# Loads that add x wait for the row of t, and ScalarE marks 18 stretches of the counts instead of 20

## The chip, the cores and the metric

The kernel runs on one core of a Trainium2 chip. The metric is the device time of one execution in microseconds (us), lower is better. TensorE multiplies matrices, VectorE and ScalarE work elementwise, GpSimd (POOL) and SyncE (SP) mainly issue transfers here.

## The reference

One layer of a graph network with attention, a spline layer behind it, a residual and a layer norm. `x` is 1250 x 512, there are 21250 edges `src -> dst` (10000 pairs both ways, and a loop on each node).

```python
HW = h @ W
s = HW @ a[:512, 0];  t = HW @ a[512:, 0]
e = leaky_relu(s[row] + t[col], 0.2)
m = segment_max(e, row);  ex = exp(e - m[row])
att = ex / segment_sum(ex, row)[row]
agg = segment_sum(att[:, None] * h[col], row)
out = silu(agg) @ base_w.T + einsum('nip,oip->no', b_splines(agg, grid), spline_w)
x = layernorm(x + out)          # h is x, row is src, col is dst
```

## The kernel before

The edges are made into a dense matrix of counts: `C[p, j, d]` says how many edges lead from node 128 j + p to node d, for ten tiles j of 128 source nodes. The work has three stages.

**Counts.** VectorE builds one-hot tiles (`hit`, `still`, `oh`, lines 540 to 590), TensorE multiplies them (line 1325) into PSUM, where 25 stretches (windows) of 50 destination nodes each lie in six banks by turns. ScalarE copies finished stretches into `C` (line 1065, ten pairs or so and single ones at the end, list `TAKEN`), and writes for each of the first `MARKED` stretches a mark `Z` (line 1070): a huge number where the count is zero, so that a maximum over `trow - Z` sees edges only. The semaphore `s_cnt` counts the copies, `s_hole` the marks. A bank may take the next stretch when the old one has been read; the wait for this stands in front of a stretch's first matmul.

**The rows of t.** At the same time TensorE works out s and t, ScalarE puts t and 0.2 t into `strow`, and SP writes them in four pieces to `t_row` in DRAM (line 410), waits for all four, and loads them back, spread over the 128 partitions: `trow` (t, line 412, semaphore `s_trow`) and `gentle` (0.2 t, line 413). SP's queue holds nothing else meanwhile.

**x in two parts.** The product with x is made of two numbers for each value: `xh`, x rounded as it is loaded, and `xl`, what is left, x - xh. For `xl` ScalarE writes minus xh (`minus_x`, line 1075, one of ten tiles after each of ten batches of edges; `s_neg` counts them), and POOL issues four loads that add x onto it in memory (lines 518 and 520): tiles 0 to 3, 4 to 6, 7 and 8, and the 98 rows of tile 9. The first signals `s_xa[0]`, the other three `s_xa[1]`. Behind them on POOL stand the loads of the weights `wh`, the first of which waits for the first aggregated tile.

**Attention.** VectorE then goes once through a loop for edges outside the bands (lines 779 to 816), in which the first tile's work is interleaved: an early maximum over the marked stretches (line 801), marks of the other stretches for tiles 0 and 1 (line 803, `NEAR`), `bent` (line 774: the leaky sums in `ex`, from gentle and trow), a late maximum over the other stretches (line 810), and then `tmax`. ScalarE takes exponentials (line 1106) and marks the other stretches of tiles 2 to 9 (`last_marks`, line 1185). TensorE transposes (line 1364) and multiplies (line 1384) for each tile three times: the high part of the weights with xh, the low part with xh, and the high part with xl. For tile 0 the product with xl comes in two parts, `sums(0, 2, 0)` for four tiles of xl, `sums(0, 2, 1)` for the other six; they wait for `s_xa[0]` and `s_xa[1]`. From there the spline layer follows (lines 1445 and 1449), in which the weights are loaded in turn.

All orders are written by hand: each engine does its instructions in the order of its program.

Of the kernel before, what the change touches and what calls it, by code (L numbers as in the profile page):

```python
# [66 lines left out]
def middle(t):  # L67


    return MID + PER_BATCH * (t // TB) + PER_TILE * (t % TB)  # L70
# [18 lines left out]
def parts_of(t):  # L89

    parts = []
    for w, lo, hi in stretches(t):
        old = min(max(reached(t, w), lo), hi) if t > FIRST_TILE[w] else lo
        parts += [(w, a, b) for a, b in ((lo, old), (old, hi)) if a < b]
    return parts
# [29 lines left out]
def build(nc, x, xT, edges, dstN, WT, a2, baseT, splT, out):  # L125
    with ExitStack() as ctx:
# [156 lines left out]

        TAKEN = [(w, 2) for w in range(0, 22, 2)] + [(22, 1), (23, 1), (24, 1)]

        MARKED, NEAR = 20, 2
        TABLE = 19

        def done(b):

            return min(TB * b + TB, NV)

        def taken(w):

            return next(k + 1 for k, (v, n) in enumerate(TAKEN) if v <= w < v + n)
# [72 lines left out]
        def lows(u):  # L368

            return sum(split_low(k) for k in range(u + 1))  # L370

        def w_source(u):
            g, h, q = units[u]
            t = baseT if q == 0 else splT[q - 1]
            return t[256 * h:256 * h + 256, :].rearrange("(c p) o -> p c o", p=128)
# [6 lines left out]
        def unit_used(u):  # L382

            if u % HU == HU - 1:
                return s_tile, 5 * (u // HU + 1)
            return s_unit, u + 1 - u // HU
# [79 lines left out]
        @block.gpsimd  # L466
        def _(e):
            e.iota(im[:, :], [[1, MV]], base=-MV // 2, channel_multiplier=0,
                   allow_small_or_imprecise_dtypes=True).then_inc(s_setup, 1)
            e.iota(mid[:, :], [[PER_BATCH, NCP // TB], [PER_TILE, TB]], base=MID, channel_multiplier=0,  # L470
                   allow_small_or_imprecise_dtypes=True).then_inc(s_setup, 1)
            e.iota(tile_of[:, :], [[1, 2]], base=0, channel_multiplier=2,
                   allow_small_or_imprecise_dtypes=True).then_inc(s_setup, 1)
            e.iota(im8[:, :], [[LANES, MV // LANES]], base=-MV // 2, channel_multiplier=0,
                   allow_small_or_imprecise_dtypes=True).then_inc(s_setup, 1)
            e.iota(lane[:, :], [[1, LANES]], base=0, channel_multiplier=0,
                   allow_small_or_imprecise_dtypes=True).then_inc(s_setup, 1)
            e.memset(nought[:, :], 0.0).then_inc(s_setup, 1)
            e.memset(ident[:, :], 0.0).then_inc(s_setup, 1)
            e.wait_ge(s_setup, SETUP["id0"])  # L480
            e.affine_select(out=ident[:, :], in_=ident[:, :], compare_op=ALU.not_equal, fill=1.0, base=0,
                            pattern=[[-1, 128]], channel_multiplier=1).then_inc(s_setup, 1)
            e.memset(xh[:, NT - 1, :].bitcast(F32), 0.0).then_inc(s_setup, 1)
            e.memset(xt0[:, :, N:RP], 0.0).then_inc(s_setup, 1)
            e.memset(bias[:, 2 * NP + 1:2 * NP + 2], BIG).then_inc(s_setup, 1)
            e.memset(ex[:, 0:3, N:RP], 0.0).then_inc(s_setup, 1)

            e.memset(half[:, :], 0.5).then_inc(s_setup, 1)
            e.memset(eps[:, :], EPS).then_inc(s_setup, 1)
            e.iota(way[:, 0, :], [[-1, 2]], base=NC, channel_multiplier=-2,  # L490
                   allow_small_or_imprecise_dtypes=True).then_inc(s_setup, 1)
            e.iota(way[:, 1, :], [[1, 2]], base=1, channel_multiplier=2,
                   allow_small_or_imprecise_dtypes=True).then_inc(s_setup, 1)
            for p in range(NP):
                e.memset(bias[:, p:p + 1], 5.5 - (p + 2)).then_inc(s_setup, 1)
            for p in range(NP):
                e.memset(bias[:, NP + p:NP + p + 1], 0.5 ** 0.5 * (5.5 - (p + 2))).then_inc(s_setup, 1)
            e.memset(bias[:, 2 * NP:2 * NP + 1], 2.0 * (1 / 6) ** 0.5).then_inc(s_setup, 1)
            e.iota(lplace[:, :, :], [[MV, LND], [0, 2]], base=MV // 2, channel_multiplier=0,
                   allow_small_or_imprecise_dtypes=True).then_inc(s_setup, 1)  # L500

            for k in range(4):
                e.memset(limit[:, 1, k:k + 1], (-1.0, 1.0, -1.0, 1.0)[k])
                e.memset(limit[:, 2, k:k + 1], (float(NC), 0.0, float(LND), 0.0)[k])
                m = e.memset(limit[:, 3, k:k + 1], (0.0, NC + 1.0, -1.0, float(LND))[k])
            m.then_inc(s_setup, 1)


            e.wait_ge(s_w, 32)
            e.wait_ge(s_setup, SETUP["rest"])  # L510
            e.dma_start(xh[:, 0:NT - 1, :], x[0:1152, :].rearrange("(w p) i -> p w i", p=128)).then_inc(s_xh, 16)
            e.dma_start(xh[0:LASTP, NT - 1, :], x[1152:N, :]).then_inc(s_xh, 16)

            for part, (lo, hi) in enumerate(zip(ADDED, ADDED[1:] + (NT - 1,))):
                e.wait_ge(s_neg, NT if hi == NT - 1 else hi)
                e.dma_start(xl[:, lo:hi, :], x[128 * lo:128 * hi, :].rearrange("(w p) i -> p w i", p=128), accum_op=ALU.add
                            ).then_inc(s_xa[min(part, 1)], 16)
            e.dma_start(xl[0:LASTP, NT - 1, :], x[1152:N, :], accum_op=ALU.add).then_inc(s_xa[1], 16)  # L520


            for u in range(NU):
                if u >= NWS:
                    e.wait_ge(*unit_used(u - NWS))
                    e.wait_ge(s_wlo, lows(u - NWS))
                elif u == 0:
                    e.wait_ge(s_agg, 1)
                elif u == 2:
                    e.wait_ge(s_agg, NT)  # L530
                e.dma_start(wh[u % NWS][:, :, :], w_source(u)).then_inc(s_wh[u % NWS], 16)  # L531
# [710 lines left out]
        def _(e):  # L1242
            def ends_along():

                e.wait_ge(s_wa, 1)
                e.wait_ge(s_tab, 9)
                e.wait_ge(s_setup, SETUP["ident"])
                e.transpose(PS[0:8, 7, 128:128 + NBLK], ends[0:NBLK, :, :].rearrange("p k j -> p (k j)"),
                            ident[0:NBLK, 0:NBLK]).then_inc(s_rt, 1)
# [52 lines left out]
            def keep_warm(n, bank=6):  # L1302

                for k in range(n):
                    e.matmul(PS[:, bank, 0:CW], nought[:, 0:128], nought[:, 0:CW], start=True, stop=True)
# [3 lines left out]
            for g, (b, n) in enumerate(GROUPS):  # L1309
                if b == BY_SCALAR:  # L1310
                    e.wait_ge(s_by, 1)
                else:
                    e.wait_ge(s_mv, g + 1 - (b > BY_SCALAR))
                e.wait_ge(s_head, g + 1)
                moved = oh8[g % RB] if IN_LANES[g] else oh_by if b == BY_SCALAR else oh[g]
                held = still[g % RB]
                for t in range(TB * b, done(b + n - 1)):
                    k, o = t - TB * b, middle(t) - REACH[b]
                    if b == BY_SCALAR and k == TB // 2:
                        keep_warm(3, 7)  # L1320
                        e.wait_ge(s_by, 2)
                    for w, lo, hi in parts_of(t):
                        if w >= 6 and lo == FIRST_OF[w] and t == FIRST_TILE[w]:
                            e.wait_ge(s_hole, taken(w - 6))
                        m = e.matmul(PS[:, w % 6, lo - CW * w:hi - CW * w], held[:, k, :], moved[:, k, lo - o:hi - o],  # L1325
                                     start=(t == FIRST_TILE[w]), stop=(t == LAST_TILE[w]))
                    m.then_inc(s_ct, 1)
                if g == 1:
                    for c in range(4):
                        w_times_a(c)  # L1330
                if g == 2:
                    wa_column()
                if g == 4:
                    ends_along()
                if g == 5:
                    most_along()
                if g in (3, 4, 5, 6):
                    st_rows(g - 3)
                if g == 9:
                    s_column()  # L1340
                if g == LOADS_AT:
                    e.wait_ge(s_tab, TABLE)
                    left = loaded(e, r_size, 4, 5, 1, LND * NC)[0]
# [177 lines left out]
```

## Time and profile before

| | |
|---|---|
| median of 3 runs | 389.68 us (388.93 to 390.03) |
| the profiled execution | 388.39 us, of which the span of the core is 386.6 |
| TensorE busy | 370.7 us (96%) |
| VectorE busy | 336.4 us (87%) |
| ScalarE busy | 255.9 us (66%) |
| POOL busy | 37.0 us (10%) |
| mean granted clock of TensorE | 0.992 |

The span is the time on the core from the first to the last instruction; all places below are counted from its start. Busy time is summed over the whole span, so it does not say which engine is waited for in a given stage.

### The profile page before, as it was taken

Reading aid. Unit: us, or ns where it says so; the run is one execution under the profiler, and the core shown is the slowest. Engines: PE = TensorE matmul, PEld = TensorE weight load, DVE = VectorE, ACT = ScalarE, POOL = GpSimd, SP = SyncE. Lnnn points to the kernel's source line nnn. Section 1 sums busy time; section 2 is a strip of 40 time slices with the busy share of each in tenths; the row PEclk is TensorE's granted clock in tenths of the full one; section 3 lists DMA queues with packets and bytes.
Section 4 is the critical chain, followed back from the end, with each engine's and each line's share of the span. In section 5 each row is a group of like instructions: output and inputs, shape, how many; then the busy total and the mean of one; then the engine's idle time right before and its main releaser. Section 6 shows DMA issues by size and latency. Waiting matters only on the chain.

```text
span 386.6 us, 5456 instructions
## 1 busy us (share of the span) xinstructions
PE 370.7 (96%) x2082; PEld 305.7 (79%) x2082; DVE 336.4 (87%) x430; ACT 255.9 (66%) x256; POOL 37.0 (10%) x92
## 2 busy tenths in 40 slices
PE   6896979999999999999999999999999999999994
PEld 3676658888888888888888888888888888888883
DVE  8997699987775789999899998988999799999445
ACT  6799454545446979774887774897667697776122
POOL 6002201000000010100101010100100101011000
PEclk9999899999999999999999999999999999999998
DMA  7918905100000047477554646442333353564202
GB/s 252 397 22 138 253 13 163 57 2 0 2 0 0 3 140 241 159 203 232 173 185 122 193 120 189 139 109 56 110 114 103 91 142 121 152 196 100 65 29 109
DMA packets 23980, 47.30 MB, mean 122 GB/s; under 512 B 1936, under 2 KB 2412, under 8 KB 23954
## 3 DMA queue, kind: packets, MB, share of 16 engines
q0 software_dynamic: 12416, 24.00, 24.2%
q1 hardware_dynamic: 11538, 22.95, 17.8%
q8 instruction: 17, 0.28, 0.3%
q14 instruction: 9, 0.07, 0.1%
HBM read 44.37 MB, written 2.57 MB: 121 GB/s over the span
## 4 chain that ended last, share of the span: by engine, by line
PE 86%; DVE 5%; DMA 4%; issue 2%; POOL 1%; ACT 1%; SPq 1%; DVEq 0%; POOLq 0%
PE PS L1449 38%; PE PS L1445 25%; PE PS L1384 18%; PE PS L1364 3%; DMA gentle<-t_row 2%; DMA t_row<-strow 1%; PE PS L1394 1%; DVE oh L574 1%; DVE still L590 1%; DVE oh L540 1%; PE PS L1459 0%; SPq L410 0%; PE PS L1325 0%; DVE hit L553 0%; DVE pat L563 0%
## 5 line engine op out<-in xcount | busy, mean ns | idle before, releaser
L1449 PE MATMUL PS<-wh,s 128*128 128x512 f32 x432 | 139.4, 390 | 0.0
L1449 PEld LDWEIGHTS PS<-wh,s 128*128 128x128 f32 x432 | 81.2, 188 | 16.8
L1445 PE MATMUL PS<-s,wh 128*128 128x482 f32 x288 | 92.8, 383 | 0.0
L1449 PE MATMUL PS<-wl,s 128*128 128x512 f32 x216 | 84.2, 390 | 0.0
L1162 ACT ACTIVATE s<-v 128x1220 fp32r<-128x1220 f32 (+1 forms) x32 | 40.0, 1250 | 37.5 <-DVE v L952 26.3
L1445 PEld LDWEIGHTS PS<-s,wh 128*128 128x128 f32 x288 | 54.6, 189 | 9.7
L1145 ACT ACTIVATE v<-xt,bias 128x1220 f32<-128x1220 f32 (+1 forms) x32 | 42.9, 1342 | 20.0 <-DVE s L962 18.0
L1445 PE MATMUL PS<-s,wl 128*128 128x482 f32 x144 | 55.2, 384 | 0.0
L946 DVE SCALAR_TENSOR_TENSOR v<-v,v 128x1220 f32<-128x1220 f32 (+1 forms) x32 | 46.4, 1450 | 7.1 <-ACT v L1148 7.1
L952 DVE SCALAR_TENSOR_TENSOR v<-v,v 128x1220 f32<-128x1220 f32 (+1 forms) x32 | 46.8, 1461 | 3.3
L962 DVE SCALAR_TENSOR_TENSOR s<-v,s 128x1220 fp32r<-128x1220 f32 (+1 forms) x32 | 46.4, 1454 | 1.3 <-ACT s L1162 1.3
L531 POOL DMA_DIRECT2D wh<-in_splT x32 | 22.9, 716 | 256.2 <-PE PS L1449 183.1
L1449 PEld LDWEIGHTS PS<-wl,s 128*128 128x128 f32 x216 | 40.5, 188 | 8.0
L948 DVE SCALAR_TENSOR_TENSOR v<-v,v 128x1220 f32<-128x1220 f32 (+1 forms) x32 | 46.5, 1453 | 0.0
L1146 ACT ACTIVATE v<-xt,bias 128x1220 f32<-128x1220 f32 (+1 forms) x32 | 42.5, 1327 | 0.0
L1148 ACT ACTIVATE v<-v,bias 128x1220 f32<-128x1220 f32 (+1 forms) x32 | 42.5, 1327 | 0.0
L1445 PEld LDWEIGHTS PS<-s,wl 128*128 128x128 f32 x144 | 27.1, 189 | 4.8
L830 DVE TENSOR_TENSOR wl<-wring,wh 128x1024 fp32r<-128x1024 f32 x24 | 29.2, 1219 | 1.5 <-issue 1.5
L1325 PEld LDWEIGHTS PS<-oh,still 128*128 128x128 bf16 x404 | 22.7, 101 | 9.7 <-DVE oh L574 7.9
L1325 PE MATMUL PS<-oh,still 128*128 128x75 fp8e4 (+38 forms) x404 | 24.6, 220 | 5.4 <-DVE oh L574 4.7
L1113 ACT CAST ph<-PS 128x1280 fp32r<-128x1280 f32 (+2 forms) x12 | 12.6, 1049 | 23.6 <-PE PS L1364 23.6
L885 DVE TENSOR_TENSOR pl<-PS,ph 128x1280 fp32r<-128x1280 f32 (+2 forms) x11 | 14.9, 1366 | 13.8 <-ACT ph L1113 13.8
(164 smaller groups left out, 429.7 us busy)
## 6 DMA issues: line engine op xcount, KB each, us to landing
wh<-in_splT POOLq DMA_DIRECT2D x32, 512.0 KB, 4.2
wring<-in_splT SPq DMA_DIRECT2D x21, 512.0 KB, 4.5
xt<-in_xT SPq DMA_DIRECT2D x1, 2500.0 KB, 12.0
xh<-in_x POOLq DMA_DIRECT2D x1, 2304.0 KB, 12.0
wh<-in_baseT POOLq DMA_DIRECT2D x4, 512.0 KB, 5.4
out<-xr SPq DMA_DIRECT2D x8, 256.0 KB
wring<-in_baseT SPq DMA_DIRECT2D x3, 512.0 KB, 3.9
xr<-in_x SPq DMA_DIRECT2D x1, 1280.0 KB, 6.4
```

The costliest lines, as they stand in the source:

```text
L946: e.scalar_tensor_tensor(out=ba, in0=bw, scalar=2.0, in1=ba, op0=ALU.subtract, op1=ALU.mult, reverse0=True).then_inc(s_a3, 1)
L948: e.scalar_tensor_tensor(out=bq, in0=bw, scalar=2.0, in1=bq, op0=ALU.subtract, op1=ALU.mult).then_inc(s_b3, 1)
L952: e.scalar_tensor_tensor(out=bw, in0=bq, scalar=2 / 3, in1=ba, op0=ALU.add, op1=ALU.min).then_inc(s_spl, 1)
L962: e.scalar_tensor_tensor(out=parts(sl, u), in0=bufs(u)[0], scalar=0.0, in1=parts(sh, u).bitcast(F32), op0=ALU.max, op1=ALU.subtract).then_ ...
L1145: e.activation(bw, agg_in, ACT.Abs, bias=bias[:, q - 1:q], scale=2.5).then_inc(s_abs, 1)
L1146: e.activation(bq, agg_in, ACT.Square, bias=bias[:, NP + q - 1:NP + q], scale=2.5 * sq2).then_inc(s_q2, 1)
L1148: e.activation(ba, bw, ACT.Square, bias=bias[:, 2 * NP:2 * NP + 1], scale=-sq6).then_inc(s_a2, 1)
L1162: e.activation(parts(sh, u), bufs(u)[0], ACT.Relu).then_inc(s_shi, 1)
L1325: m = e.matmul(PS[:, w % 6, lo - CW * w:hi - CW * w], held[:, k, :], moved[:, k, lo - o:hi - o], start=(t == FIRST_TILE[w]), stop=(t == LA ...
L1384: m = e.matmul(PS[:, 5 + j % 2, :], pp[:, j % 3, place(j, t), :], xs[:, t % NT, :], start=(i == 0 and t == 0), stop=(i == end and t == b - ...
L1445: m = e.matmul(PS[:, w, 0:TURNED], wx[:, ic, 128 * w:128 * w + 128], sx[:, ic, 0:TURNED], start=begins, stop=ends_)
L1449: m = e.matmul(PS[:, out_bank(w), :], sx[:, ic, c:c + 128], wx[:, ic, :], start=begins, stop=ends_)
```

## The change

Two constants of the program and one wait. POOL waits for `trow` before the first of its four adding loads; the loads themselves and their order stay. `MARKED` is 18: ScalarE makes no mark for the pair of stretches 18 and 19 while the counts are made, and these two stretches go with the last five, to VectorE for tiles 0 and 1 and to ScalarE's `last_marks` for the others. A stretch whose old bank has no mark any more waits for the copy (`s_cnt`); of the 25 this is stretch 24, which follows stretch 18.

```diff
-        MARKED, NEAR = 20, 2
+        MARKED, NEAR = 18, 2
...
+            e.wait_ge(s_trow, 16)
             for part, (lo, hi) in enumerate(zip(ADDED, ADDED[1:] + (NT - 1,))):
                 e.wait_ge(s_neg, NT if hi == NT - 1 else hi)
                 e.dma_start(xl[:, lo:hi, :], x[128 * lo:128 * hi, :].rearrange("(w p) i -> p w i", p=128), accum_op=ALU.add
...
                         if w >= 6 and lo == FIRST_OF[w] and t == FIRST_TILE[w]:
-                            e.wait_ge(s_hole, taken(w - 6))
+                            e.wait_ge(s_hole if w - 6 < MARKED else s_cnt, taken(w - 6))
```

POOL's program around the loads, with the semaphores that a row waits for (`a_neg` is `s_neg`, `a_trow` is `s_trow`, `t_agg` is `s_agg`); before:

```order
L512 DMA xh<-in_x 98x512
L518 DMA xl<-in_x 128x4x512 [waits a_neg]
L518 DMA xl<-in_x 128x3x512 [waits a_neg]
L518 DMA xl<-in_x 128x2x512 [waits a_neg]
L520 DMA xl<-in_x 98x512
L531 DMA wh_107<-in_baseT 128x2x512 [waits t_agg]
```

and now (the new line shifts all line numbers behind it by one):

```order
L512 DMA xh<-in_x 98x512
L519 DMA xl<-in_x 128x4x512 [waits a_neg,a_trow]
L519 DMA xl<-in_x 128x3x512 [waits a_neg]
L519 DMA xl<-in_x 128x2x512 [waits a_neg]
L521 DMA xl<-in_x 98x512
L532 DMA wh_107<-in_baseT 128x2x512 [waits t_agg]
```

The order is the same; the first load has one more wait, and the other three stand behind it.

ScalarE's program at the end of the counts, where the pairs of stretches 18 and 19 and 20 and 21 are copied (`t_ct` counts the count matmuls); before:

```order
L1065 CAST C<-PS 128x10x100 [waits t_ct]
L1070 ACTIVATE Z<-PS,bias 128x10x100
L1075 ACTIVATE xl<-xh 128x512 [waits s_xh]
L1087 ACTIVATE s_part<-PS 128x3 [waits t_sc]
L1087 ACTIVATE s_part<-PS 128x3
L1087 ACTIVATE s_part<-PS 128x2 x2
L1065 CAST C<-PS 128x10x100 [waits t_ct]
```

and now:

```order
L1066 CAST C<-PS 128x10x100 [waits t_ct]
L1076 ACTIVATE xl<-xh 128x512 [waits s_xh]
L1088 ACTIVATE s_part<-PS 128x3 [waits t_sc]
L1088 ACTIVATE s_part<-PS 128x3
L1088 ACTIVATE s_part<-PS 128x2 x2
L1066 CAST C<-PS 128x10x100 [waits t_ct]
```

The mark is gone, and what stood behind it follows the copy.

VectorE's program in its loop, from the early maximum (`scrap` with its result `top`) to the late one; before:

```order
L764 ISA scrap,top<-trow,Z 128x1000 [waits v_touch,a_scol,a_hole,a_trow]
L764 ISA top 128x1
L719 TENSOR_SCALAR Z<-C 128x2x250 [waits a_cnt]
L774 SCALAR_TENSOR_TENSOR ex<-gentle,s_part,trow 128x512 [waits a_gentle,a_scol,a_trow]
L808 ISA [waits v_near,t_ovp,v_early]
L808 TENSOR_TENSOR C<-C,PS 128x10x32
L764 ISA scrap,top<-trow,Z 128x250
```

and now:

```order
L765 ISA scrap,top<-trow,Z 128x900 [waits v_touch,a_scol,a_hole,a_trow]
L765 ISA top 128x1
L720 TENSOR_SCALAR Z<-C 128x2x350 [waits a_cnt]
L775 SCALAR_TENSOR_TENSOR ex<-gentle,s_part,trow 128x512 [waits a_gentle,a_scol,a_trow]
L809 ISA [waits v_near,t_ovp,v_early]
L809 TENSOR_TENSOR C<-C,PS 128x10x32
L765 ISA scrap,top<-trow,Z 128x350
```

The instructions and their waits are the same; 100 columns have moved from the early maximum to the late one, and the marks of two tiles have grown from 250 columns to 350.

## Rows read from the trace of the kernel before

**Rows 1.** The page, chain that ended last: share of the span by engine.

```profile
PE 86%; DVE 5%; DMA 4%; issue 2%; POOL 1%; ACT 1%; SPq 1%; DVEq 0%; POOLq 0%
```

**Rows 2.** Chain of waits: start, length (us), what; three pieces from 29 to 47.

```profile
29.22 0.66 SPq L410
...
31.10 5.70 DMA t_row<-strow
...
37.22 9.38 DMA gentle<-t_row
```

**Rows 3.** Timeline of VectorE: start, length (us), instruction, [idle before it, releaser].

```profile
35.94 0.46 DVE L553 TENSOR_TENSOR hit<-im,gk 128x544 f16<-128x544 f16 x1 [2.16 <-issue]
...
41.50 0.32 DVE L793 TENSOR_TENSOR one_moving<-im,kk 128x320 bf16<-128x320 f16 x1
44.82 1.20 DVE L764 CUSTOM_DVE_ANT_0 scrap<-trow,Z 128x1000 bf16<-128x1000 f32 x1 [3.00 <-DMA trow<-t_row]
...
45.95 0.29 DVE L719 TENSOR_SCALAR Z<-C 128x500 bf16<-128x500 uint16 x1
46.72 0.75 DVE L774 SCALAR_TENSOR_TENSOR ex<-gentle,s_part,trow 128x512 f32<-128x512 f32 x1 [0.48 <-DMA gentle<-t_row]
```

**Rows 4.** Timeline of ScalarE: marks, the last copies, the cast after last marks.

```profile
38.12 1.19 ACT L1070 ACTIVATE Z<-PS,bias 128x1000 bf16<-128x1000 f32 x1
...
43.58 1.07 ACT L1065 CAST C<-PS 128x500 uint16<-128x500 f32 x2 [0.38 <-PE PS L1325]
...
57.17 2.13 ACT L1185 ACTIVATE Z<-C,bias 128x250 bf16<-128x250 uint16 x2
60.21 1.23 ACT L1113 CAST ph<-PS 128x1280 fp32r<-128x1280 f32 x1 [0.90 <-PE PS L1364]
```

**Rows 5.** Timeline of TensorE (PE matmuls, PEld weight loads): counts, products with xl, transposes.

```profile
38.79 5.25 PE L1325 MATMUL PS<-oh,still 128*128 128x211 fp8e4 x74 [1.84 <-DVE oh L574]
...
55.72 2.45 PE L1384 MATMUL PS<-xl,ph 128*128 128x512 f32 x10
...
58.83 1.10 PEld L1364 LDWEIGHTS PS<-ident,ex 128*128 128x128 f32 x10 [0.18 <-DVE ex L863]
```

**Rows 6.** Tile xl: POOL's issues, ns min/median/max, first and last start (us).

```profile
L518 POOL DMA_DIRECT2D xl<-in_x x3: 1194/1290/1352, 28.7 to 40.1; - x3
L520 POOL DMA_DIRECT2D xl<-in_x x1: 1363/1363/1363, 40.9 to 40.9; - x1
```

**Rows 7.** DMA queues in 29.5:30.7, 30.7:34.5, 34.5:36.5, 37:40.5, 41.5:45: packets, MB, share.

```profile
q1 hardware_dynamic: 4, 0.00, 0.9%
...
q0 software_dynamic: 260, 0.53, 102.0%
...
q1 hardware_dynamic: 12, 0.01, 1.7%
...
q0 software_dynamic: 311, 0.61, 104.1%
...
q1 hardware_dynamic: 231, 1.09, 99.7%
```

**Rows 8.** DMA issues of the whole run: KB each, us from issue to landing.

```profile
wring<-in_baseT SPq DMA_DIRECT2D x3, 512.0 KB, 3.9
...
xl<-in_x POOLq DMA_DIRECT2D x1, 1024.0 KB, 8.9
...
trow<-t_row SPq DMA_DIRECT2D x1, 640.0 KB, 8.0
...
ei<-in_edges SPq DMA_DIRECT2D x1, 176.0 KB, 2.4
```

**Rows 9.** Windows: stretch, its length, busy us (instructions), PEclk, DMA share, GB/s.

```profile
29.00:30.00 1.00, 1.00 (x19) 0.78 (x16) 1.00 (x5) 1.00 (x3) 1.00 (x1) 1.00 0.08 16
39.50:42.50 3.00, 3.00 (x36) 2.88 (x35) 2.32 (x8) 1.57 (x6) 2.11 (x2) 0.50 1.12 281
46.00:48.00 2.00, 2.00 (x11) 0.89 (x10) 1.52 (x6) 0.00 (x0) 0.00 (x0) 1.00 1.14 208
```

## The prediction

> **What bounds the kernel now.** I read the page's chain of work first: 86% of it is TensorE [rows 1]. From about 54 us to the end TensorE hardly pauses, so whatever makes that stream begin sooner or later moves the end by as much. Then I read the chain of waits just ahead of the stream: two transfers stand in it, the last row written to t_row (issued at 31.10, landed 5.70 later) and `gentle` (issued at 37.22, landed at 46.60) [rows 2]. VectorE's timeline shows what they hold up: it is through with the one-hots at 41.82, waits 3.00 for trow, does the early maximum (1.20) and the near marks (0.29), waits 0.48 for gentle, and at 46.72 begins `bent`, from which everything up to the stream follows [rows 3]. The other input of this stretch, the counts, is complete when ScalarE's last copy ends, 43.58 + 1.07 = 44.65 [rows 4]. So the rows of t are late by about two microseconds against the counts.
>
> Why they are late is seen in the DMA queues. POOL issues the loads that add x at 28.74 and on to 40.87 [rows 6]; their packets are in q0, those of t_row, trow and gentle in q1. The first write of t_row has its 4 packets through between 29.5 and 30.7. From 30.7 to 34.5 there are q0 packets alone, at 102% of the 16 engines, and the other 12 packets of t_row come only between 34.5 and 36.5. It happens again to trow: issued at 36.81, it has no packet from 37.0 to 40.5, where q0 alone fills the engines, and q1 gets them (99.7%) from 41.5 on [rows 7]. So a q1 packet here waits for what q0 has queued before it.
>
> **The wait on POOL.** It holds back four loads. Behind them on POOL stand only the weight loads, which wait for the first aggregated tile anyway, so nothing else is late by it; SP's queue is not changed, but what it issues no longer meets the loads. Its effect in steps:
>
> *The rows of t.* The last write is issued at 31.10. Its packets should come some 1.4 later, as those of the first write did (issued at 29.22 [rows 2], through by 30.7 [rows 7]), and it lands between 33.0 (0.5 after its packets) and 33.5 (2.4 after issue, as `ei` does [rows 8]). Then trow: 640 KB. The lower end is 3.9, what a 512 KB load takes [rows 8]; the upper is 1.5 to the first packet, 0.655 MB at the 311 GB/s that q1 had from 41.5 to 45 (1.09 MB in 3.5 us [rows 7]) = 2.1, and 0.9 for landing = 4.5. So trow lands at T = 36.9 to 38.0; I take 37.5, against 44.8 before (36.81 + 8.0). gentle, issued 0.4 behind it, takes its turn on the same engines: some 2 us more, 39.5, against 46.60.
>
> *VectorE.* The early maximum no longer waits: it runs from 41.85 to about 43 in what was idle time. The near marks need all counts, 44.65. They take 0.29 for 2x250 [rows 3]; 2x350 at the same price per element is 0.41, so they end at 45.1. bent starts there, 46.72 - 45.1 = 1.6 sooner. The late maximum grows from 250 to 350 columns; at the early one's 1.20 for 1000 that is 0.12, on the path. The sum at the row maximum, and so at TensorE's stream: **1.5 us sooner**. What is late next is the counts, then TensorE's own stream.
>
> *The loads themselves.* I put them at nothing only if they land before TensorE wants them. It wants the second part (all four loads) at the fifth of ten matmuls on xl, 55.72 + 4 x 0.23 = 56.6, the weights 0.2 before: 56.4; 1.5 sooner that is 54.9 [rows 5]. Alone, the loads move 208 GB/s at 114% share [rows 9]. At that the first one's 1.05 MB take 5.0 of its 8.9 from issue to landing [rows 8], so 3.9 are start and landing; all four together, 2.56 MB, take 12.3, and I put 12.8, that is 200 GB/s, to leave room for pauses between the loads. Together T + 16.7: 54.2 for T = 37.5, and 53.6 to 54.7 over the bounds. They are hidden with 0.7 to spare (0.2 at the upper bound); each microsecond beyond that is paid in full, but for 0.18 that TensorE waits soon after in any case [rows 5]. The first part lands after 8.9, at 46.4, far ahead of the 54.0 at which it is wanted.
>
> **The marks.** Gone is one Z mark of ScalarE, 1.19 at 38.12 [rows 4]. It gives nothing: ScalarE waits for TensorE before the next counts. It comes back later as 800 more elements in the last marks, 2.13 for 2000, so 0.85 more; ahead of the next cast ScalarE stands idle 0.90 there [rows 4], which hides it (if the cover were short, tile 1's cast and TensorE behind it would be late by the rest, at most 0.3). TensorE's wait for the bank of stretch 24 now goes by the copy instead of the mark; that copy stands ahead of the mark, which began at 38.12, and the matmuls that need it belong to the run of 74 that TensorE begins at 38.79 [rows 5]: nothing. The costs of near marks and late maximum, 0.1 each, are in the sum above.
>
> The profiled execution took 388.39, so it would take 386.9; it lies 1.29 under the median of the runs shown, and from that, 389.68, I predict **388.2**. From runs between 388.93 and 390.03, 0.3% (1.17 us) is about what can be told from no change.
>
> **A rule that speaks against it.** While POOL issued the first load, from 29 to 30 us, VectorE was busy all the time, and POOL's issue ended after 1.35 as usual [rows 6, 9]; the load at 40.87, half of it beside an idle VectorE, took 1.36. So VectorE did not hold POOL up. The Trainium skill (SBUF — State Buffer, section "SBUF: two separate sides") says that GpSimd writes the descriptors of such a DMA itself and is locked out while VectorE runs an instruction that takes both port pairs; by that rule, if VectorE's instructions here are such, loads held together into VectorE's busiest stretch could stand still there. The rows do not bear it out, and the sum goes by the rows.
>
> **The rivals.**
> *The rows of t come no sooner* (slower). If the write lands at 36.8 as before, because t_row itself is slow and not because of q0, trow follows 4.2 later, T = 41.0, and the loads end at 57.7. TensorE then stands still from 54.9, 2.8 less 0.18 = 2.6; against 1.5 gained that is 1.1 lost. Before, after a wait of 1.84 for VectorE, its granted clock was 0.50 (1.2 GHz) for the 3 us from 39.5 [rows 5, 9]; another such stretch costs 1.5 more: 392.3, or 390.8 without. The point from which it decides is T = 39.9, where the stall eats the gain. Against it: the first write's packets in rows 7, which went through before q0 was busy. 7 in 100.
> *The loads are late by a little.* T between 38.7 and 39.9, or a slower q0: 388.5 to 389.7. The spare 0.7 is thin. 13 in 100.
> *gentle meets the loads.* They are issued when trow lands, gentle perhaps still on its way; were it held as trow was held from 37 to 40.5, it would land 3.5 to 5 later, 43 to 44.5 or, if later still, behind the counts, with up to all of the gain lost: 388.5 to 389.7. Against it: gentle was issued 0.4 behind trow and needs its engines for 2, and the loads spend a part of their 3.9 before their first packets. 8 in 100.
> *POOL is held up by VectorE* (slower): as the rule above would have it, issue waits until 42.95, the early maximum's end; the loads end at 43 + 16.7 = 59.7, a stall of 4.8 less 0.18, so 3.1 lost: 392.8. 2 in 100.
> *The counts end sooner too.* Before its last three groups VectorE stands 2.16 in front of a `hit` [rows 3] for values it loads into registers. If the loads of x slow that, VectorE and TensorE gain up to 2, TensorE also the half clock behind its wait, and the time is then set by the landing at 54.2: 56.4 - 54.2 + 0.2 = 2.4 sooner, 387.3 (386.7 for T = 36.9). No row shows that these values come through the DMA engines. 10 in 100.
>
> **How the numbers follow.** The forecast has the other 60 in 100, by itself 387.8 to 388.6. 0.3% under the median is 388.5: nearly all of the forecast and the last rival, and a little of the two small delays, 0.62 faster; the two slower rivals and a clock lost in a small stall, 0.11; the rest, 0.27, the same. The range takes in the two delays and the sooner counts, 386.9 to 389.8, and leaves out the two slower rivals.
>
> **What would show it.** Right: no q0 packet until trow lands; t_row's packets within 2 us of their issue; trow landed by 38.5 and gentle by 41; the early maximum at about 41.9 without a wait; near marks waiting for the counts at 44.7; bent at 45.1; no pause of TensorE ahead of its matmuls on xl; ScalarE's last marks about 3 us and its cast still released by TensorE. Wrong: a wait of TensorE for a DMA at 55 us, or a trow that still takes 8 us with q0 empty.

## The result and the profile after

The changed kernel takes 385.69 us (median of 7 runs, 385.38 to 387.50) against 389.03 for the kernel before (7 runs, 388.32 to 390.03), run beside it. The ratio of the means, 386.36 to 389.14, is 0.9928, with a 95% interval of 0.9904 to 0.9953. That is 0.72% or 2.8 us faster. The forecast was 1.5 us faster (388.2, range 386.9 to 389.8): the direction was right, the gain about half of what came, and the median lies under the range. Two single runs of the sections below, one of the kernel before at 395.47 and one of the fifth experiment at 483.97, had a lower mean clock than the others and are left out of all ratios.

The seven runs fall into two groups: four at 385.4 to 385.7, with a mean granted clock of TensorE of 0.996 to 0.999, and three at 387.4 to 387.5, with 0.992. The profiled execution, 387.50 with a span of 385.7, is one of the second group, so it is only 0.9 shorter than the 388.39 of the profiled execution before; the fifth experiment comes to that.

First the page's chain that ended last, its share by engine, and the chain of waits from 34 to 60 us. Answers to [rows 1, 2].

```profile
PE 85%; DMA 9%; ACT 4%; POOL 1%; DVE 1%; SPq 0%; issue 0%; DVEq 0%
37.42 2.45 POOL xl L519 x2
39.87 14.11 DMA xl<-in_x
53.98 0.04 issue
54.02 3.50 PE PS L1385 x10
```

DMA has gone from 4% to 9%. t_row and gentle are gone from the chain; the last of the four adding loads, issued at 39.87 and landed at 53.98, now releases TensorE. The timeline of VectorE (start, length, instruction, idle before it and releaser), as in [rows 3]:

```profile
33.70 0.44 DVE L554 TENSOR_TENSOR hit<-im,gk 128x544 f16<-128x544 f16 x1
...
39.49 1.08 DVE L765 CUSTOM_DVE_ANT_0 scrap<-trow,Z 128x900 bf16<-128x900 f32 x1
...
41.67 0.34 DVE L720 TENSOR_SCALAR Z<-C 128x700 bf16<-128x700 uint16 x1 [1.09 <-ACT C L1066]
41.92 0.75 DVE L775 SCALAR_TENSOR_TENSOR ex<-gentle,s_part,trow 128x512 f32<-128x512 f32 x1
```

The early maximum waits no more for trow. But the `hit` before it has also moved, from 35.94 to 33.70, and its wait of 2.16 is gone: all VectorE's work from there on is 2.2 sooner. `bent` begins at 41.92 instead of 46.72. ScalarE's timeline, as in [rows 4], and TensorE's, as in [rows 5]:

```profile
39.05 2.59 ACT L1066 CAST C<-PS 128x1000 uint16<-128x1000 f32 x4
...
52.48 2.80 ACT L1186 ACTIVATE Z<-C,bias 128x350 bf16<-128x350 uint16 x2
59.34 1.23 ACT L1114 CAST ph<-PS 128x1280 fp32r<-128x1280 f32 x1 [4.06 <-PE PS L1365]
```

```profile
37.30 3.72 PE L1326 MATMUL PS<-oh,still 128*128 128x211 fp8e4 x74 [0.36 <-DVE still L591]
...
51.00 1.07 PE L1385 MATMUL PS<-xl,ph 128*128 128x512 f32 x4
54.02 1.79 PE L1385 MATMUL PS<-xl,ph 128*128 128x512 f32 x6 [1.96 <-DMA xl<-in_x]
...
57.32 1.99 PE L1365 MATMUL PS<-ident,ex 128*128 128x128 f32 x10
```

The counts end at 39.05 + 2.59 = 41.64, 3.0 sooner than the 44.65 of before. Half of that is TensorE's last run of 74 count matmuls, which begins 1.5 sooner, and half that the run takes 3.72 instead of 5.25. TensorE then comes to the second part of xl so soon that it stands still for 1.96. The queues in 30.7:34 and 37:40.5, the landings, and two windows (stretch; length; busy PE, PEld, DVE, ACT, POOL; granted clock; DMA share; GB/s), as in [rows 7 to 9]:

```profile
q1 hardware_dynamic: 12, 0.01, 0.7%
...
q0 software_dynamic: 4, 0.01, 1.4%
```

```profile
trow<-t_row SPq DMA_DIRECT2D x1, 640.0 KB, 4.4
gentle<-t_row SPq DMA_DIRECT2D x1, 625.0 KB, 5.6
xl<-in_x POOLq DMA_DIRECT2D x1, 196.0 KB, 14.1
```

```profile
37.30:41.00 3.70, 3.70 (x76) 3.66 (x77) 3.27 (x9) 3.65 (x10) 3.58 (x4) 1.00 0.30 78
54.10:60.10 6.00, 6.00 (x25) 4.99 (x26) 3.09 (x6) 1.94 (x2) 0.00 (x0) 0.72 0.01 3
```

The last 12 packets of t_row pass between 30.7 and 34 (before, between 34.5 and 36.5), and trow, issued at 32.69, lands 4.4 later instead of 8.0. TensorE's granted clock is full in the stretch of the last counts, where it had been half (1.2 of 2.4 GHz) in [rows 9]; behind TensorE's new wait it is 0.72 over 6 us.

### The profile page after: what moved, and what is told of

The parts are those of the page before. It is cut to its first block, busy times and chain, and to the rows that moved or that the text cites. A ratio compares the mean times of both kernels' runs of the same rounds, so it can differ in the third digit from the quotient of the medians.

```text
span 385.7 us, 5456 instructions
## 1 busy us (share of the span) xinstructions
PE 371.6 (96%) x2082; PEld 305.9 (79%) x2082; DVE 336.4 (87%) x430; ACT 255.4 (66%) x255; POOL 37.1 (10%) x92
## 4 chain that ended last, share of the span: by engine, by line
PE 85%; DMA 9%; ACT 4%; POOL 1%; DVE 1%; SPq 0%; issue 0%; DVEq 0%
PE PS L1450 38%; PE PS L1446 25%; PE PS L1385 17%; DMA xl<-in_x 4%; DMA xh<-in_x 3%; PE PS L1365 3%; DMA av<-in_a 2%; ACT Z L1071 1%; ACT xl L1076 1%; ACT C L1066 1%; PE PS L1395 1%; POOL xl L519 1%; PE PS L1460 0%; POOL xh L511 0%; DVE st L978 0%
## 5 line engine op out<-in xcount | busy, mean ns | idle before, releaser
L1163 ACT ACTIVATE s<-v 128x1220 fp32r<-128x1220 f32 (+1 forms) x32 | 40.0, 1250 | 37.5 <-DVE v L953 26.3
L1450 PEld LDWEIGHTS PS<-wl,s 128*128 128x128 f32 x216 | 40.5, 188 | 8.0
L1385 PE MATMUL PS<-xl,ph 128*128 128x512 f32 x100 | 25.9, 404 | 2.0 <-DMA xl<-in_x 2.0
L1326 PEld LDWEIGHTS PS<-oh,still 128*128 128x128 bf16 x404 | 21.4, 97 | 6.8 <-DVE oh L575 5.9
```

What stands on the lines that cost most here:

```text
L1163: e.activation(parts(sh, u), bufs(u)[0], ACT.Relu).then_inc(s_shi, 1)
L1385: m = e.matmul(PS[:, 5 + j % 2, :], pp[:, j % 3, place(j, t), :], xs[:, t % NT, :], start=(i == 0 and t == 0), stop=(i == end and t == b - ...
L1450: m = e.matmul(PS[:, out_bank(w), :], sx[:, ic, c:c + 128], wx[:, ic, :], start=begins, stop=ends_)
```

## The experiments

Theory A: the values that VectorE and TensorE load into registers before the last groups of edges are slow while the adding loads' packets are under way; the wait on POOL takes the packets out of that place, so the counts end sooner too. Theory B: the mark that ScalarE no longer makes lets the counts end sooner. A third question (C) was what sets the end now: the landing of xl, or something behind it. A measure for C in every trace is where TensorE begins its products of tile 1 with xh (61.49 before, 60.62 now): in all 17 profiled executions the measured time is that place plus 326.7 to 326.9 us, so what differs between these kernels differs ahead of it. Diffs are against the changed kernel unless the text says otherwise. Three kernels do other arithmetic: in the seventh and the fifteenth the loads do not add, so `xl` holds x and not x - xh; the sixth takes five sizes as constants that the others read from the data.

**One: the wait alone.**

```diff
-        MARKED, NEAR = 18, 2
+        MARKED, NEAR = 20, 2
```

> The wait on POOL alone, MARKED stays 20. Theory A (VectorE's register values come slowly while the adding loads fill the DMA engines; without them the counts end 3 us sooner, and TensorE then waits for the loads): as the change, VectorE's 2.16 us in front of its hit is gone, the counts end near 41.7, TensorE waits for xl until about 54.0, 385.4 to 387.5 us. Theory B (the mark that ScalarE no longer makes lets the counts end sooner): the counts end near 44 and most of the gain is gone, 388 us or more.

Measured: 385.82, ratio 0.9919 (0.9901 to 0.9938). `hit` at 33.70 has no wait. From the timelines of ScalarE, VectorE and TensorE:

```profile
40.07 2.56 ACT L1066 CAST C<-PS 128x1000 uint16<-128x1000 f32 x4
...
42.66 0.29 DVE L720 TENSOR_SCALAR Z<-C 128x500 bf16<-128x500 uint16 x1 [0.95 <-ACT C L1066]
...
54.18 1.65 PE L1385 MATMUL PS<-xl,ph 128*128 128x512 f32 x6 [1.28 <-DMA xl<-in_x]
```

The whole gain is there with all marks made, so B falls as its cause. The mark does make the last copies 1.0 later (they run to 42.63, against 41.64), which TensorE's wait for xl swallows: tile 1's products begin at 59.15, 2.3 sooner than before.

**Two: the marks alone.**

```diff
-            e.wait_ge(s_trow, 16)
             for part, (lo, hi) in enumerate(zip(ADDED, ADDED[1:] + (NT - 1,))):
```

> MARKED = 18 alone, POOL does not wait. Theory A: trow lands at 44.8 and gentle at 46.6 as before, VectorE's 2.16 us stays; the late maximum is 0.1 longer: 389.0 to 389.3 us, no difference from before that can be told. Theory B: the counts end about 3 us sooner, though trow hides it; VectorE's 2.16 us is gone.

Measured: 390.21, ratio 1.003 (1.0017 to 1.0043), a little slower, where no difference was expected. VectorE's timeline, and TensorE's last counts:

```profile
36.21 0.46 DVE L553 TENSOR_TENSOR hit<-im,gk 128x544 f16<-128x544 f16 x1 [2.43 <-issue]
...
48.51 0.75 DVE L774 SCALAR_TENSOR_TENSOR ex<-gentle,s_part,trow 128x512 f32<-128x512 f32 x1 [1.71 <-DMA gentle<-t_row]
```

```profile
39.05 3.73 PE L1325 MATMUL PS<-oh,still 128*128 128x211 fp8e4 x74 [2.11 <-DVE oh L574]
```

ScalarE, one mark ahead, has minus x ready sooner, POOL issues the third adding load at 39.41 instead of 40.12, and gentle now takes 11.2 to land. So it looks as if a saving on ScalarE releases a transfer into the way of another; the two were not tried apart. One more thing is to be seen here: after a wait of 2.11 TensorE's 74 matmuls take 3.73, at the full clock, while in [rows 5] they take 5.25 after 1.84. So the half clock of the kernel before is not there in every execution that has the wait.

**Three: POOL waits for the write of t_row only.** `s_tline` counts the four writes of t_row.

```diff
-            e.wait_ge(s_trow, 16)
+            e.wait_ge(s_tline, 64)
```

> POOL waits for the written t_row (the semaphore on which SP issues trow), not for the landed trow: its loads are issued at 32.7 instead of 37.4. If TensorE's wait at 52 to 54 us is for the loads alone (theory A), they land near 49.5, the wait is gone, TensorE's matmuls on xl run through at 51, and the time is 383 to 384 us, if gentle is not held up. If q0's packets push gentle back (packets of q0 from about 35.7, gentle's still under way), gentle lands up to 5 us later, at 43, and 1 to 2 us of that is lost: 385 us. Theory C (the end is set by something behind xl, such as the transposes of tile 1): no faster than the change's faster runs, 385.4.

Measured: 384.83, ratio 0.9891 (0.9873 to 0.9908), about 1 us under the changed kernel. TensorE:

```profile
52.82 1.66 PE L1385 MATMUL PS<-xl,ph 128*128 128x512 f32 x6 [0.74 <-DMA xl<-in_x]
```

The loads land 1.2 sooner, at 52.8, not the 4.4 by which they are issued sooner (32.98 for 37.42), and not at 49.5 as expected: now their packets stand behind those of trow and gentle and begin at 38.5, as those of t_row and trow stood behind the loads before. The landing of xl is what TensorE waits for, and moving it moves the time (C: the landing). Tile 1's products begin at 57.80, 3.7 sooner than before, and the profiled time, 384.69, is 3.7 shorter.

**Four: POOL waits until VectorE has its values** (the eighth `hit` of the one-hots), and for nothing else.

```diff
-            e.wait_ge(s_trow, 16)
+            e.wait_ge(s_hit, 8)
```

> POOL waits for VectorE's eighth hit, the first one behind VectorE's register values, at 34.1: 3 us sooner than trow lands, and behind the issue of trow and gentle. Theory A: register values and rows of t are out of the way, the loads land near 50.9, just ahead of the 51.7 at which TensorE wants them; no wait of TensorE, no half clock: 383.3 to 383.8 us. Theory C: 385.4 or more.

Measured: 385.54, ratio 0.9905 (0.9887 to 0.9924): no better than the change, and the expectation missed. TensorE no longer waits for xl, but its last counts are late:

```profile
38.32 5.24 PE L1326 MATMUL PS<-oh,still 128*128 128x211 fp8e4 x74 [1.37 <-DVE oh L575]
```

Its wait is put down to an `oh` that VectorE makes from 37.20 to 37.84, but in the changed kernel the same matmuls begin at 37.30, beside it. TensorE loads one register value at this place, and the loads' first packets are now just there; the half clock (5.24 for the 74, as in [rows 5]) follows its wait. That this value is what was slow is argued from the place; six, which has no such value, bears it out.

**Five: TensorE kept busy in its wait**, by nine matmuls of zeros behind the first part of xl, ahead of the wait.

```diff
             sums(0, 2, 0)
+            keep_warm(9)
             sums(0, 2, 1)
```

> The change, with nine idle matmuls (0.21 us each, into a bank not yet in use) ahead of TensorE's wait for the second part of xl, 2 us of work in place of standing still. If the 387.4 us runs differ from the 385.5 us runs by TensorE's clock alone, all runs are near 385.5 now and the granted clock behind the wait stays 1.00. If they differ by when the loads land, 387.4 us appears again.

Measured: 385.66 over three runs (385.51 to 385.81), ratio 0.9914 (0.9893 to 0.9936). Window 54.1 to 60.1:

```profile
54.10:60.10 6.00, 6.00 (x32) 4.77 (x32) 4.39 (x7) 3.64 (x3) 0.90 (x2) 1.00 0.04 9
```

The clock is full where it was 0.72, and none of the three runs is near 387.4. Together with the clocks of the seven runs (0.992 in each of the slower three) this says that the second group of the changed kernel's runs is the half clock behind the wait for xl: 1.9 us between the groups, of which 1.6 is seen in the trace (from the second part of xl to tile 1's products it is 6.60, and 4.97 in one, at the full clock). That the nine matmuls are what keeps the clock up is not shown: in ten, without them, none of six runs is near 387.4 either.

**Six: the kernel before, with constants in place of register values** (the values are the same, so the work is).

```diff
-                    first, tiles, first_win, many, left = (
-                        within(v, *ends) for v, ends in zip(loaded(e, r_size, 0, 5, 0, LND * NC), (
-                            (0, NC), (1, NC + 1), (0, LND - 1), (1, LND), (1, LND * NC))))
+                    first, tiles, first_win, many, left = NC, 1, LND - 1, 1, 1
...
-                    left = loaded(e, r_size, 4, 5, 1, LND * NC)[0]
+                    left = 1
```

> The kernel before with the five values of VectorE's loop and the one of TensorE's written into the program as constants, not loaded into registers (the loops run once, as they do with these inputs). Theory A (register values slowed by the loads): VectorE's 2.16 us in front of its hit is gone, the counts end near 41.7 to 42.5, but trow still lands at 44.8 and gentle at 46.6, so the time stays at 388.5 to 389.3. Theory D (VectorE waits there for something else that the transfers slow): the 2.16 us stays and the counts end at 44.7.

Measured: 388.91, ratio 1.0002 (0.9991 to 1.0012). VectorE:

```profile
33.69 0.44 DVE L553 TENSOR_TENSOR hit<-im,gk 128x544 f16<-128x544 f16 x1
...
45.03 1.20 DVE L762 CUSTOM_DVE_ANT_0 scrap<-trow,Z 128x1000 bf16<-128x1000 f32 x1 [5.50 <-DMA trow<-t_row]
```

The 2.16 before `hit` are the register values (VectorE's wait on the semaphore in front of them is kept), and the counts end at 42.36. TensorE, without its one value, begins its last counts at 36.85 and has no wait; it begins them at 37.30 in the changed kernel and at 38.32 in four. Alone that is worth nothing: the early maximum waits 5.50 for trow instead of 3.00. Only with the rows of t out of the way does it pay, and the wait on POOL does both.

**Seven: the kernel before, with loads that do not add.**

```diff
-                e.dma_start(xl[:, lo:hi, :], ..., accum_op=ALU.add
+                e.dma_start(xl[:, lo:hi, :], ...
```

> The kernel before with the four loads of x as plain loads, without adding (so xl holds x, and the results are others). If it is the adding that fills the engines, the same bytes take about half the time (some 400 GB/s in place of 208), t_row's last write and trow land 2 to 3 us sooner each, and 1 to 1.5 us is gained: 387.5 to 388 us. If any load in q0 does the same harm, t_row lands at 36.8 and trow at 44.8 as before: 389 us.

Measured: 384.83, ratio 0.9908 (0.9876 to 0.9941), some 3 us better than expected: `hit` is on time as well. The queue in 32:33.5, and VectorE:

```profile
q0 software_dynamic: 294, 0.60, 123.3%
```

```profile
33.70 0.44 DVE L553 TENSOR_TENSOR hit<-im,gk 128x544 f16<-128x544 f16 x1
```

The plain load moves 0.60 MB in 1.5 us, 400 GB/s, in the very stretch ahead of `hit`, and `hit` has no wait. Bytes alone do not slow the values here; loads that add do. trow takes 4.1 here, without any wait on POOL.

**Eight: the second part of xl last** of tile 0's products (`end = 2` closes the sum there).

```diff
-                end = 2 if j else 1
+                end = 2
...
-            sums(0, 2, 1)
             sums(0, 1, 0)
             turn(1)
             sums(0, 1, 1)
+            sums(0, 2, 1)
```

> The change, with TensorE's second part on xl moved behind the low products and the transposes of tile 1. Theory A: TensorE no longer stands still from 52.1 to 54.0; it waits about 1 us for VectorE's weights of tile 1 at 54.1 instead, and finishes tile 0 about 0.9 us sooner: 384.5 us, with the clock kept. If the loads are not the bound there, 385.4 to 387.5 as the change.

Measured: 384.95, ratio 0.99 (0.9879 to 0.9921), near the 384.5 of theory A.

```profile
54.46 1.31 PE L1365 MATMUL PS<-ident,ex 128*128 128x128 f32 x10 [1.13 <-DVE ex L864]
```

The wait for the loads is gone from TensorE; a smaller one for VectorE, 1.13, stands in its place.

**Nine: three, with four of the low products ahead of xl's second part.**

```diff
-            e.wait_ge(s_trow, 16)
+            e.wait_ge(s_tline, 64)
...
-            sums(0, 2, 1)
             sums(0, 1, 0)
+            sums(0, 2, 1)
             turn(1)
```

> The early wait of e3_tline, and TensorE's first low products (four matmuls, 0.9 us) put ahead of its second part on xl. In e3_tline TensorE waited 0.74 us for the loads, which landed at 52.8; now it has work until 52.9. If the loads are what is left of the bound (theory A), the wait is gone and the time is 0.7 us under e3_tline's 384.8: 384.1. If VectorE's weights of tile 1 (done at 54.1) are the bound by now, nothing is gained: 384.8.

Measured: 384.67, ratio 0.9882 (0.9866 to 0.9898), 0.16 from three, which can't be told apart; theory A's 384.1 is not confirmed by the times.

```profile
51.92 1.10 PE L1385 MATMUL PS<-xh,pl 128*128 128x512 f32 x4
52.97 1.66 PE L1385 MATMUL PS<-xl,ph 128*128 128x512 f32 x6
```

TensorE no longer waits for xl, and in the profiled execution (383.95) tile 1's products begin at 57.05, 0.75 sooner than in three (0.7 was expected). What is left before its long stream is its own work.

**Ten: the changed kernel again**, with no edit.

> The change itself once more, beside the others on one chip: 385.4 to 387.5 us as measured, the slower runs with the lower granted clock, if the half clock behind TensorE's wait comes and goes from run to run.

Measured: 386.37, ratio 0.9918 (0.99 to 0.9935), runs from 384.96 to 386.54. The slower runs here do not show a lower clock, against the expectation:

```profile
54.59 1.66 PE L1385 MATMUL PS<-xl,ph 128*128 128x512 f32 x6 [1.57 <-DMA xl<-in_x]
```

In this profiled execution VectorE is 0.93 later from its first `still` on (6.25 instead of 5.32; a `hit` at 31.64 that stood at 30.71), and xl's second part begins at 54.59 instead of 54.02; the clock is full behind that wait. So not all of the spread of the change is the half clock.

**Eleven and twelve: the values loaded late,** behind VectorE's last group, in three and in the changed kernel. There the first instruction behind them is `kk`.

```diff
-                if g == LOADS_AT:
+                if g == NG - 1:
```

> e3_tline with VectorE's five register values loaded three groups later, at about 38.6 instead of 33.7, when packets of the adding loads flow (from 38.7 there). Theory A: VectorE now stands still in front of its loop, about 2 us, the near marks come at 43 to 43.5 in place of 41.7, and some 1 us is lost against e3_tline: 385.8 us. If the values are not slowed by such packets: under 1 us of standing still, as in e12_change_late_values, and 384.8 us.

> The change with the same move of VectorE's register values; here the first adding packets come at 40.0 to 40.5, behind the values. Theory A: VectorE stands still 1 us or less in front of its loop, and TensorE's wait for xl hides it: as the change, 385.4 to 387.5 us.

Measured: 384.54 (0.9881, 0.9859 to 0.9903) and 385.63 (0.9909, 0.9887 to 0.9931), each near its parent (384.83 and 385.69). VectorE, in eleven and in twelve:

```profile
40.13 0.16 DVE L788 TENSOR_TENSOR kk<-left_key,lplace 128x2 f16 x1 [1.03 <-issue]
```

```profile
40.96 0.16 DVE L788 TENSOR_TENSOR kk<-left_key,lplace 128x2 f16 x1 [1.87 <-issue]
```

This was the reverse of what was expected: eleven has the adding packets in flow here (from 38.5 on) and the smaller wait, twelve has few packets, while POOL is issuing (37.17 to 42.0). So a second reading came up: it is POOL's issuing that slows the values (Q), not the packets (P). Eleven speaks against Q too: POOL issues its last two loads from 39.10 to 41.2 there, beside the same wait.

**Thirteen: twelve, with the loads held back behind `tmax`,** so that neither is there.

```diff
-            e.wait_ge(s_trow, 16)
+            e.wait_ge(s_tmax, 1)
```

> VectorE's register values behind its last group as in e12, and POOL's loads only when the first row maximum is done (about 45), so that neither their issue nor their packets stand beside the values. It gives the standing still that belongs to the late place itself, where less work covers the values. If the 1.03 us of e11 is that cover alone, 1.0 us here too; if packets made up part of it, less. The time is of no use (loads land near 61): 393 us or so.

```profile
40.14 0.16 DVE L788 TENSOR_TENSOR kk<-left_key,lplace 128x2 f16 x1 [1.01 <-issue]
```

The late place costs 1.01 by itself, so the loads add nothing in eleven and 0.86 in twelve. The time, one run of 394.81, shows what late loads cost: TensorE waits 2.87 and 5.62 for the two parts of xl.

**Fourteen: the kernel before, with the first load where it was and the others issued late.** Against the kernel before:

```diff
-                e.wait_ge(s_neg, NT if hi == NT - 1 else hi)
+                e.wait_ge(s_neg, hi if lo == 0 else NT)
```

> The kernel before, with the second load issued together with the third (at 40): the packets of the first load flow from 32 to 37 as before, but POOL issues nothing between 30.1 and 40. Theory P (adding packets in flight slow the register values): VectorE's 2.16 us in front of its hit stays. Theory Q (POOL's issuing slows them, in the kernel before that of 34.81 to 36.10): under 1 us. Time near that of before or a little over it, 388 to 390 us, since trow meets fewer packets and the loads land later.

The timelines of POOL and VectorE, and the queue in 32:37:

```profile
28.74 1.35 POOL L518 DMA_DIRECT2D xl<-in_x  x1 [18.54 <-ACT xl L1075]
40.13 2.52 POOL L518 DMA_DIRECT2D xl<-in_x  x2 [10.03 <-ACT xl L1075]
```

```profile
35.94 0.46 DVE L553 TENSOR_TENSOR hit<-im,gk 128x544 f16<-128x544 f16 x1 [2.16 <-issue]
...
44.64 0.29 DVE L719 TENSOR_SCALAR Z<-C 128x500 bf16<-128x500 uint16 x1 [1.71 <-ACT C L1065]
44.85 0.74 DVE L774 SCALAR_TENSOR_TENSOR ex<-gentle,s_part,trow 128x512 f32<-128x512 f32 x1
```

```profile
q0 software_dynamic: 494, 0.99, 108.9%
```

POOL issues nothing from 30.1 to 40.1, and the wait of 2.16 is there unchanged: so here the loads under way make it, not the issuing (P). It also gives a run of the forecast's own scene: rows of t in time, counts as before, no wait for xl. Near marks wait for the counts at 44.64 and `bent` begins at 44.85; forecast were 44.65 and, with the longer marks of the change, 45.1. TensorE:

```profile
53.82 2.45 PE L1384 MATMUL PS<-xl,ph 128*128 128x512 f32 x10
```

That is 1.9 before the 55.72 of [rows 5]. Its one run took 386.31, 2.1 less than the profiled execution of the kernel before and under the 388 to 390 that were expected: the loads, though later, were still in time.

**Fifteen: twelve, with loads that do not add** (the edit of seven).

> e12_change_late_values with plain loads in place of adding ones (so xl holds x). POOL issues from 37.2 here too, four loads of about 0.75 us in place of 3.9 us together and more. If it is POOL's issuing of any load that slows the values (theory Q), VectorE stands still 1.5 to 1.9 us as in e12; if it is the adding loads, no more than in e13, about 1 us. Loads land near 46, TensorE does not wait: 383.5 to 384.5 us.

```profile
40.12 0.16 DVE L788 TENSOR_TENSOR kk<-left_key,lplace 128x2 f16 x1 [1.01 <-issue]
```

One run, 383.64. POOL issues from 37.16 on, though each load for a shorter time than in twelve, and the 0.86 are gone: again only loads that add slow the values.

## Why the prediction was wrong

**The step that failed** is "The near marks need all counts, 44.65". The rows of t were taken away from the front, and the next thing behind them was left where it stood. But it stood there partly because of the same loads: from 31 to 36 us they slowed the register values (fourteen: 2.16 with packets and no issuing; seven: none with plain loads; six: none without the values), and TensorE's last counts were late by that wait and by the half clock behind it. With the wait on POOL the counts end at 41.64, 3.0 sooner, of which TensorE's earlier begin is 1.49 and its full clock 1.53; by two, that second half need not be there in every run of the kernel before. What is late next is then not the counts but the landing of xl, which the sum had as hidden with 0.7 to spare. The prediction had this as its last rival, at 10 in 100 and 387.3 ("the time is then set by the landing at 54.2"); the landing came at 53.98, TensorE went on at 54.02. It was priced low because no row showed that the values had to do with DMA. That was so, but a wait of 2.16 whose releaser is only "issue", in the very stretch in which the change empties a queue, was a price that could move, and it deserved more than 10.

**The size.** For the scene it was made for, the sum was good: without the longer marks it gives 1.8, and fourteen has 1.9. In the changed kernel `bent` is 4.8 sooner and TensorE wants xl's second part at 54.02 - 1.96 = 52.1, 4.5 before the 56.6 of the old kernel; 2.6 of that is left when the loads land, where the rival had 2.4. So of the 3.0 by which the counts are sooner some 0.7 gets through. In the profiled execution 1.6 of the 2.6 is lost again behind the wait: 6 us at a mean clock of 0.72, with the ten transposes at 57.32 taking 1.99 where those of five and ten take 1.25.

The 2.8 of the times is an average: the four quicker runs are 3.6 under the mean of the kernel before, the three others 1.7. That 3.6 is more than the traces explain, since the kernel before was traced in one of its quicker runs (388.39); what its slower runs wait for was not looked at. The 388.2 also started from 389.68, the median of three runs, and beside the change it was 389.03.

**What held.** q0 is empty until trow lands (4 packets from 37 to 40.5, all behind it). t_row landed by 32.69, 33.0 to 33.5 forecast; trow at 37.1 (37.5); gentle at 38.7 (39.5). The loads landed at 53.98, that is trow's landing + 16.9, where 16.7 was forecast. The early maximum has no wait. ScalarE's last marks take 2.80 (about 3), and the cast behind them still waits for TensorE. "No pause of TensorE ahead of its matmuls on xl" failed, as the failed step makes it; the wait of TensorE for a DMA, named as a sign of being wrong, came at 52.1 instead of 55.

**The marks.** "It gives nothing: ScalarE waits for TensorE" holds of the kernel before, not of the one that came: in one, with the mark, ScalarE's copies run back to back from 40.07 and end 1.0 later than without it. The loads hide that. Without the wait on POOL the marks cost 0.3% or 1.2 (two), of which the sum had 0.2.

**The rule on the port.** POOL issued the four loads between 37.42 and 42.24 beside a VectorE that was busy for 3.27 of the 3.7 us from 37.30; 4.8 for four is no more than the 1.2 to 1.4 each of [rows 6]. (The load at 40.87 in the kernel before, which the prediction took to be half beside an idle VectorE, was so for a third, from 41.82 to 42.23.) The Trainium skill (SBUF — State Buffer, section "SBUF: two separate sides") says that POOL cannot write the descriptors of its loads while VectorE runs an instruction that takes both port pairs; that did not show here either, but no run shows that VectorE's instructions in this stretch were of that kind.

**Open.** How loads that add slow the values is not settled. Nor is why twelve, with 49 GB/s at a DMA share of 1.58 between 39.0 and 39.5, lost 0.86 and eleven nothing; the values may have been read in eleven before the flow began, which was not measured. Unless that is so, adding packets in flow are not by themselves enough. And the engines being full is not the whole of why t_row waits: in the kernel before no packet of either queue passes from 31.2 to 31.8, and the 12 packets come only after 34.5.

## What to carry to other kernels

Before the gain of a removed wait is capped by what is late next, ask whether that, too, is held by what is being moved: a wait with no visible releaser in the same stretch is the first suspect. A load held back to clear the way is free only until the cleared engine wants its data, so its landing goes into the sum as the new bound, and of two waits that clear the way the lesser one (here for the write of t_row, not for the load of trow) let the loads land 1.2 sooner. An experiment on one part of a change can show a loss that the whole hides, so each part is run alone.

## What the runs showed of the hardware

- Loads that add move 208 GB/s here with the 16 engines at 113 to 114% (46 to 48 us before, 45 to 51 us after); the same loads without adding, 400 GB/s (seven).
- Values loaded into registers cost VectorE 2.16 more while adding loads were under way (before, fourteen), and nothing more beside plain ones at twice the rate (seven); at a later place they cost 1.01 by themselves, 0.86 more in twelve and nothing more in eleven, with adding loads under way in both.
- A queue's packets wait behind what the other had queued, both ways: 12 small ones of t_row until 34.5 in [rows 7], and the loads' own in three, issued at 32.98 and begun at 38.5.
- After a wait of 1.96 TensorE's granted clock was 0.72 over the next 6 us in one execution; after one of 1.57 in another of the same kernel (ten) it stayed full. After 1.84 it was 0.50 in [rows 9], after 2.11 (two) it stayed full.
